# Two expert stages: when the second tile is turned, how long unread products run, and when the last quarter of a weight matrix is loaded

## The chip, the cores and the metric

The kernel runs on one core of a Trainium2 chip, as one program. The metric is the device time of one execution in microseconds (us). TensorE is called PE, VectorE DVE, ScalarE ACT, GpSimd POOL and SyncE SP, as in the profile.

## The reference, cut to what matters

Two transformer layers over x of 4096 tokens by 256 channels, each an attention and a feed-forward part made of eight experts. Every token goes to one expert. Only the feed-forward parts matter here:

```python
# layer 0: every token to the centroid that scores it highest
aff = x @ centroids.T; assign = argmax(aff, 1); alpha = sigmoid(aff[assign])
h = relu(layernorm(x, ln_g[e], ln_b[e]) @ w1[e].T + b1[e])     # 256 -> 1024
ye = x + h @ w2[e].T + b2[e]                                   # 1024 -> 256
out = alpha * ye + (1 - alpha) * x
# layer 1: top-capacity selection, then for the expert of each token
h = gelu(x @ W1[e]) @ W2[e]                                    # 256 -> 512 -> 256
out = weight * h
```

All of it is in float32.

## The kernel before, in words

The tokens are sorted by expert on the chip. For each layer a *plan* finds the place of each token and inverts the sorting: `invert_dve` builds one-hot matrices on DVE in four batches, and `invert_pe` multiplies them on PE, batch after batch, each waiting on `p_low`. The result, read by DVE in `keep_tokens`, is `tok_i`: which token sits in which row of which 128-row tile. Then comes an *expert stage*, a software pipeline over tiles (39 in layer 0 in `expert_stage`, 34 in layer 1 in `f1_*`). All engines run their own instruction streams in program order and meet through semaphores.

For tile j the work is: POOL fetches 128 rows of 3 KB from DRAM by `tok_i` (indirect DMA, L1173 and L1899; at most six tiles ahead); PE turns the rows (`turn_in`, two transposes, L1198 and L1916); ACT copies the turned rows to SBUF (L1359, with scale and bias; L1979 in layer 1); DVE copies the first matrix of the tile's expert into `w_now` (L1303, 128x2048; L2016 in layer 1); PE multiplies (`up`, 32 matmul records, L1210; 16, L1932); ACT applies relu (L1365) or gelu (L1987); PE multiplies by the second matrix (`down`, L1224, L1955), read in place from `whi` in layer 0; DVE adds, scales and normalises; POOL stores.

In layer 0, PE's program order at the start is: turn 0, up 0, turn 1, turn 2, up 1, down 0, up 2, down 1, and so on. Because `w_now` is a single buffer, DVE refills it for tile 1 in two halves: the first when half of up 0 is done (L1297, semaphore `half`), the second when all of it is (L1303). ACT's order is: copy 0, copy 1, relu 0, copy 2, relu 1. In layer 1, `w_now1` is double, and the order is: turn 0, up 0, turn 1, turn 2, up 1, down 0.

`hold_clock(n)` issues n matmuls of the identity into a bank that nobody reads, which the profile records as 2n matmuls of line L287. It stands before the stage (25 in both layers) and before `invert_pe` (30 in layer 0, 34 in layer 1).

SP issues all direct DMAs in one program order, on one queue. `whi` takes the second matrices of layer 0 (1 MB for an expert) in six loads on the semaphore `s_w2`: experts 0, 1, 2 and 4 during the attention, and in `plan0_sync` expert 3 and then experts 5 to 7 in one load of 3 MB. Behind them, once the last normalised rows are stored, come four loads on `s_bias`: two scale and shift vectors, the first bias `b1T`, and the second bias spread over 128 partitions (`b2bc`, 1 MB, L1078). Then SP waits for the third turned tile (`tin` at 3) and loads the next layer's weights. `waits0` says what each stream waits for as it starts: DVE for `s_bias` and the first matrices (`s_w1`), ACT for `s_bias`, PE ahead of down 0 for all of `s_w2`.

Of the kernel before, what the change touches and what calls it, by code (L numbers as in the profile page):

```python
# [68 lines left out]
def two_layer_kernel(nc, a):  # L69
    ctx = ExitStack()  # L70
    with ctx:
# [66 lines left out]
        s_x, s_cst, s_w1, s_w2, s_wa, s_wb, s_modbc = (sem(n) for n in ("s_x", "s_cst", "s_w1", "s_w2", "s_wa", "s_wb", "s_modbc"))  # L138
# [27 lines left out]
        dve = {}  # L166
# [146 lines left out]
        def batches(count):  # L313
            return min(count, B)

        W2_LOADS = 6

        def load_w2(eng, e, count=1):

# [750 lines left out]
        def plan0_sync(eng):  # L1070
            eng.wait_ge(ev["aff"], scored(B - 1))
            load_w2(eng, 3)
            load_w2(eng, 5, 3)
            eng.wait_ge(s_fin, 16 * (2 + 2 * B))
            eng.dma_start(g0T, a["ln_gT"]).then_inc(s_bias, 16)
            eng.dma_start(be0T, a["ln_bT"]).then_inc(s_bias, 16)
            eng.dma_start(b1T, a["b1T"]).then_inc(s_bias, 16)
            eng.dma_start(b2bc, a["b2"].unsqueeze(0).broadcast_to([P, E, D])).then_inc(s_bias, 16)  # L1078

        def plan0_vector(eng):  # L1080
            ch = dve["chain"]
# [54 lines left out]
        def expert_stage(layer, tag, cv, cx, src_d, dst_d, rounds_before, w_up, w_down, nf, prep_in, hidden_act, bias_row, waits):  # L1136
# [48 lines left out]

            def on_tensor(eng):
                waits(eng, "tensor")
                hold_clock(eng, 25)
                eng.wait_ge(p_tok, layer + 1)

                def turn_in(t):
                    if normed and t.by_blocks():
                        return
                    eng.wait_ge(s_in[t.slot], (t.rounds + 1 + rounds_before[t.slot]) * 16)
                    if t.after(1):
                        eng.wait_ge(e_["inT"], t.j - 1 if normed and t.after(3) else t.j)
                    for c in range(C):
                        last = eng.transpose(b_in[:, c * P:(c + 1) * P], xin[t.slot][:, c * P:(c + 1) * P], ident)  # L1198
                    last.then_inc(e_["tin"], 1)

                def up(t):
                    eng.wait_ge(e_["inT"], t.j + 1)
                    eng.wait_ge(e_["w"], t.j + (2 if t.after(1) else 1))
                    if t.after(2):
                        eng.wait_ge(e_["act"], t.j - 1)
                    for f in range(nf):
                        if t.static and t.j == 1 and f == nf // 2:
                            eng.wait_ge(e_["w"], 3)
                        for c in range(C):
                            last = eng.matmul(b_up[t.par][f // 4][:, (f % 4) * P:(f % 4 + 1) * P], w_now[:, c, f * P:(f + 1) * P],  # L1210
                                              inT[t.par][:, c * P:(c + 1) * P], start=c == 0, stop=c == C - 1)
                        if t.static and t.j == 0 and f == nf // 2 - 1:
                            last.then_inc(e_["half"], 1)
                    last.then_inc(e_["up"], 1)

                def down(t):
                    e = expert_of(eng, t)
                    eng.wait_ge(e_["act"], t.j + 1)
                    if not t.after(1):
                        waits(eng, "down")  # L1220
                    if t.after(2):
                        eng.wait_ge(e_["sum"], t.j - 1)
                    for f in range(nf):
                        last = eng.matmul(b_dn[t.par][:, 0:D], hidT[t.par][:, f * P:(f + 1) * P],  # L1224
                                          w_down[:, bass.ds(e, 1), f, :].rearrange("p o n -> p (o n)"),
                                          start=f == 0, stop=f == nf - 1)
                    last.then_inc(e_["dn"], 1)
                def turn_rest(t):
                    if not t.static or t.j != 1:
                        turn_in(t)  # L1230

                def turn_second(t):
                    if t.static and t.j == 1:
                        turn_in(t)
                pipeline(eng, [(ahead, turn_rest), (ahead + 1, up), (ahead, turn_second), (ahead + 2, down)], head)

            def on_scalar(eng):
                eng.wait_ge(p_tok, layer + 1)
# [32 lines left out]
            def on_vector(eng):  # L1271
# [33 lines left out]
                def out_rows(t):  # L1305
                    total = fout[t.par][:, wide - D:wide]
                    ffn = b_dn[t.par][:, 0:D]
                    if normed:
                        e = expert_of(eng, t)
                    eng.wait_ge(e_["dn"], t.j + 1)  # L1310
                    eng.wait_ge(s_in[t.slot], (t.rounds + 1 + rounds_before[t.slot]) * 16)
                    if t.after(2):
                        eng.wait_ge(s_st[t.par], t.pairs * 16)
                    settle(eng)
                    if normed:
                        eng.tensor_tensor(total, ffn, bias_row(e), ALU.add).then_inc(e_["b"], 1)
                        eng.wait_ge(e_["b"], t.j + 1)
                        settle(eng)
                        ffn = total
                    eng.scalar_tensor_tensor(total, ffn, slot_w[:, bass.ds(t.j, 1)], xin[t.slot][:, 2 * D:], ALU.mult, ALU.mult).then_inc(e_["y"], 1)  # L1320
                    eng.wait_ge(e_["y"], t.j + 1)
                    eng.tensor_tensor(total, total, xin[t.slot][:, D:2 * D], ALU.add).then_inc(e_["sum"], 1)
                    if normed:
                        st_, mv_, _ = ln[t.par]
                        eng.wait_ge(e_["sum"], t.j + 1)
                        settle(eng)
                        eng.bn_stats(st_, total).then_inc(e_["bs"], 1)
                        eng.wait_ge(e_["bs"], t.j + 1)
                        settle(eng)
                        eng.bn_aggr(mv_, st_).then_inc(e_["mv"], 1)  # L1330
# [13 lines left out]
        def waits0(eng, who):  # L1344
            if who == "sync":
                eng.dma_start(wqkv1, a["wqkv1"]).then_inc(s_wa, 16)
                for k in range(TB):
                    eng.dma_start(wfc[k * 32:(k + 1) * 32].rearrange("r j n -> r (j n)"), a["wfc"]).then_inc(s_wa, 16)
                eng.dma_start(wg, a["wg"]).then_inc(s_wa, 16)
            elif who in ("vector", "scalar"):  # L1350
                eng.wait_ge(s_bias, 64)
                if who == "vector":
                    eng.wait_ge(s_w1, 16)
            elif who == "down":
                eng.wait_ge(s_w2, 16 * W2_LOADS)

# [550 lines left out]
        def f1_tensor(eng):  # L1907
# [11 lines left out]
            def up(t):  # L1919
                eng.wait_ge(g_["inT"], t.j + 1)  # L1920
                wait_some(eng, g_["act"], t.j - 1)
                if t.mixed:
                    eng.wait_ge(g_["unit"], 2 * STRIPS * (t.nth + 1))
                    for c in range(C):
                        for k, u in enumerate(t.strips):
                            last = eng.matmul(b_up1[t.par][u, :], inT1[t.par][:, c * P + u.start:c * P + u.stop], unit_up[t.nth % 2][:, k, c, :],  # L1926
                                              start=c == 0, stop=c == C - 1)
                else:
                    eng.wait_ge(g_["w"], t.full + 1)
                    for f in range(NF1):  # L1930
                        for c in range(C):
                            last = eng.matmul(b_up1[t.par][:, f * P:(f + 1) * P], w_now1[t.full % 2][:, c, f * P:(f + 1) * P],  # L1932
                                              inT1[t.par][:, c * P:(c + 1) * P], start=c == 0, stop=c == C - 1)
                last.then_inc(g_["up"], 1)
# [24 lines left out]
            def step(at):  # L1959
                now, second, third, fourth = (at(lag) for lag in range(4))  # L1960
                if now and now.j != 1:
                    turn_in(now)
                if second:
                    up(second)
                if now and now.j == 1:
                    turn_in(now)
                if fourth and fourth.mixed:
                    down(fourth)
                if third:
                    (turn_hidden if third.mixed else down)(third)  # L1970
# [88 lines left out]
        with nc.Block() as block:  # L2059
# [5 lines left out]

            @block.vector
            def _(eng):
                ch = Chain(eng, "s_vq")
                ch.do(eng.tensor_reduce(mx, key3, AX.X, ALU.max))
                eng.tensor_tensor(key3, key3, bc_last(mx, E), ALU.subtract).then_inc(q_key, 1)  # L2070
                for i, n in enumerate(ODD + EVEN + (0,)):
# [71 lines left out]
            def _(eng):  # L2143
# [19 lines left out]
                hold_clock(eng, 18)  # L2163
                eng.wait_ge(p_one, 2)
                prefix_pe(eng, onehot, p_pre)
                hold_clock(eng, 34)
                invert_pe(eng, 1).then_inc(p_inv, 1)
                f1_tensor(eng)

# [54 lines left out]
```

## Time and profile before

| | |
|---|---|
| three timed runs | 1011.42, 1015.40, 1015.35 us; median 1015.35 |
| profiled execution | 1017.07 us, span of the core 1015.1 us |
| mean granted PE clock | 0.975 |
| busy share of the span | PE 93%, weight loads 78%, DVE 69%, ACT 48%, POOL 32% |
| layer 0's expert stage | first rows fetched at 226.3 us, last products about 496 us |
| layer 1's expert stage | first rows fetched at 862.9 us, end of the span 1015.1 us |

The span runs from the first to the last instruction of the profiled execution; the 1.97 us between it and that execution's time lie outside the instructions. Times in the timelines are counted from the span's start. A granted clock of 1.00 is 2.4 GHz, 0.50 is 1.2 GHz.

### The profile page before, as it was taken

To read this page: it belongs to the slowest core of one execution; us is meant where nothing else is said; L and a number is where in the kernel's file an instruction comes from. 1 tells how busy PE (TensorE), PEld (TensorE's weight loads), DVE (VectorE), ACT (ScalarE), POOL (GpSimd) and SP (SyncE) were. 2 spreads that over 40 slices of the span, in tenths; PEclk is the share of its full clock that TensorE was granted. 3 is DMA by queue.
4 is the path that set the end of the run, shared out by engine and by line. 5 is a ranking of instruction groups with operands and counts; after the bars stand their busy time and mean duration, and the time that the engine had idled before them with its cause. 6 is when DMAs were issued, how large, how long until landed. Compare 5 with 4: busy or idle time off the path is not lost. (4 is left out here: it accounts for less than half of the span.)

```text
span 1015.1 us, 29867 instructions
## 1 busy us (share of the span) xinstructions
PE 941.4 (93%) x11226; PEld 793.5 (78%) x11227; DVE 705.3 (69%) x1820; ACT 491.7 (48%) x1325; POOL 321.5 (32%) x288
## 2 busy tenths in 40 slices
PE   6899999987999999999999999999878889999996
PEld 3466666887999999999987778888767778888875
DVE  3567887873777777777640679899888777466662
ACT  3646565312545444454534868788762440222221
POOL 0034533612232323323120334434433000555562
PEclk9999999998999999999999999999999897999998
DMA  9884581285322223222116757766642710443440
GB/s 337 233 329 120 126 269 70 85 309 192 95 89 85 90 88 98 78 94 87 45 40 117 132 104 156 144 148 141 118 106 70 310 65 1 138 135 117 140 139 32
DMA packets 130474, 133.76 MB, mean 132 GB/s; under 512 B 73693, under 2 KB 118879, under 8 KB 128181
## 3 DMA queue, kind: packets, MB, share of 16 engines
q1 hardware_dynamic: 119764, 90.82, 32.3%
q0 software_dynamic: 10592, 41.30, 12.7%
q8 instruction: 82, 1.34, 0.6%
q14 instruction: 36, 0.29, 0.1%
HBM read 94.27 MB, written 44.11 MB: 136 GB/s over the span
## 5 line engine op out<-in xcount | busy, mean ns | idle before, releaser
L1210 PE MATMUL psall<-rows 128*128 128x128 f32 x1248 | 148.2, 278 | 1.7 <-DVE rows L1303 1.7
L1210 PEld LDWEIGHTS psall<-rows 128*128 128x128 f32 x1248 | 146.3, 195 | 2.9 <-ACT rows L1359 1.9
L1224 PE MATMUL psall<-whi,rows 128*128 x624 | 141.0, 379 | 0.0
L1224 PEld LDWEIGHTS psall<-whi,rows 128*128 128x128 f32 x624 | 115.7, 190 | 14.1
L1178 POOL DMA_INDIRECT attn_rows<-rows,tok_i x39 | 41.7, 1069 | 183.6 <-DVE rows L1335 183.6
L287 PE MATMUL psall<-cst 128*128 128x128 f32 x718 | 93.8, 289 | 0.6 <-PEq L1451 0.6
L1570 DVE STREAM_TRANSPOSE whi<-whi 32x512 f32<-32x512 f32 x128 | 89.9, 702 | 5.9 <-POOL whi L1529 3.8
L287 PEld LDWEIGHTS psall<-cst 128*128 128x128 f32 x718 | 89.5, 204 | 1.4 <-issue 1.1
L1303 DVE COPY rows<-wlo 128x2048 f32 (+1 forms) x39 | 47.3, 1214 | 58.1 <-PE psall L1210 49.4
L1365 ACT ACTIVATE rows<-psall,vs 128x128 f32<-128x128 f32 x312 | 84.6, 382 | 4.5 <-PE psall L1210 2.1
L1649 ACT ACTIVATE whi<-psall 32x512 f32<-32x512 f32 x128 | 75.1, 587 | 12.7 <-PE psall L1814 10.5
L1899 POOL DMA_INDIRECT x<-ffn_rows,tok_i x34 | 38.8, 1142 | 123.2 <-DVE tok_i L1057 74.3
L1741 PE MATMUL psall<-wlo,x 128*32 128x128 f32 x2048 | 65.6, 280 | 2.0 <-issue 1.9
L1741 PEld LDWEIGHTS psall<-wlo,x 128*32 128x32 f32 x2048 | 56.1, 113 | 12.0 <-issue 11.1
L1266 ACT ACTIVATE small<-small,eps_t 128x1 f32<-128x1 f32 x39 | 11.5, 295 | 107.0 <-DVE small L1330 107.0
L1529 POOL TENSOR_TENSOR whi<-whi,wlo 128x512 f32<-128x512 f32 x32 | 34.0, 1063 | 89.5 <-DVE wlo L1561 89.5
L773 PE MATMUL psall<-whi 128*128 128x512 f32 x128 | 58.0, 597 | 1.1 <-ACT key L679 1.1
L1173 POOL DMA_INDIRECT x<-ffn_rows,tok_i x39 | 40.0, 1025 | 52.8 <-issue 34.1
L1932 PE MATMUL psall<-rows 128*128 128x128 f32 x448 | 54.7, 275 | 0.5 <-ACT rows L1979 0.5
L1955 PE MATMUL psall<-wlo,rows 128*128 x224 | 54.0, 385 | 0.0
L1932 PEld LDWEIGHTS psall<-rows 128*128 128x128 f32 x448 | 52.3, 192 | 0.8 <-ACT rows L1979 0.8
L1979 ACT ACTIVATE rows<-psall 128x256 f32<-128x256 f32 x34 | 13.1, 385 | 78.1 <-PE psall L1916 78.1
(299 smaller groups left out, 1842.7 us busy)
## 6 DMA issues: line engine op xcount, KB each, us to landing
ffn_rows<-mod_rows SPq DMA_DIRECT2D x2, 4096.0 KB
wlo<-attn_rows SPq DMA_DIRECT2D x64, 128.0 KB, 3.3
wlo<-in_W SPq DMA_DIRECT2D x2, 4096.0 KB, 17.7
whi<-in_w SPq DMA_DIRECT2D x5, 1024.0 KB, 8.7
whi<-mod_rows SPq DMA_DIRECT2D x4, 1024.0 KB, 14.0
ffn_rows<-rows SPq DMA_DIRECT2D x8, 512.0 KB
ffn_rows<-x SPq DMA_DIRECT2D x8, 512.0 KB
v_turn<-wlo SPq DMA_DIRECT2D x32, 128.0 KB, 3.2
```

Source lines behind the costliest of these rows:

```text
L287: eng.matmul(b_idle, ident, ident, start=True, stop=True)
L773: last = eng.matmul(ps[k % 2][:, :], h0T[:, c, k * P:(k + 1) * P], wqkv[:, c, D:3 * D], start=c == 0, stop=c == C - 1)
L1178: eng.indirect_dma_start(dst_d, bass.IndirectOffsetOnAxis(tok_i[:, j:j + 1].bitcast(U32), 0), fout[j % 2], None, bounds_check=T - 1, oob_i ...
L1210: last = eng.matmul(b_up[t.par][f // 4][:, (f % 4) * P:(f % 4 + 1) * P], w_now[:, c, f * P:(f + 1) * P], inT[t.par][:, c * P:(c + 1) * P], ...
L1224: last = eng.matmul(b_dn[t.par][:, 0:D], hidT[t.par][:, f * P:(f + 1) * P], w_down[:, bass.ds(e, 1), f, :].rearrange("p o n -> p (o n)"), ...
L1303: eng.tensor_copy(w_now[:, :, part], w_of_e[:, :, part]).then_inc(e_["w"], 1)
L1365: last = eng.activation(dst[:, f * P:(f + 1) * P], banks[f // 4][:, (f % 4) * P:(f % 4 + 1) * P], ACT.Relu, bias=b1T[:, f, bass.ds(e, 1)])
L1570: last = eng.transpose(ebd[t % 2][rows_q, :, 32 * q:32 * q + 32], sc[t % 3][rows_q])
L1649: last = eng.activation(sc[t % 3][rows_q], b_s[rows_q, :, 32 * q:32 * q + 32], ACT.Copy)
L1741: last = eng.matmul(b_qk[t % 2][k * QD:(k + 1) * QD, n * P:(n + 1) * P], wqkv1[:, c, h * QD:(h + 1) * QD], hT[b % 2][:, c, k * P:(k + 1) * ...
L1932: last = eng.matmul(b_up1[t.par][:, f * P:(f + 1) * P], w_now1[t.full % 2][:, c, f * P:(f + 1) * P], inT1[t.par][:, c * P:(c + 1) * P], st ...
L1955: last = eng.matmul(b_dn1[t.par][:, 0:D], hidT1[t.par][:, f * P:(f + 1) * P], w_down1[:, bass.ds(e, 1), f, :].rearrange("p o n -> p (o n)" ...
```

## The change

1. `plan0_sync` loads expert 5 alone. Experts 6 and 7 (2 MB, "the last quarter") are asked for after the four bias loads and after a wait for the rows of tile 1 (`s_in[1]`). There are seven loads on `s_w2`.
2. Layer 0's stage holds with 30 unread products, not 25; layer 1's plan with 40, not 34. The hold of 25 at the start of layer 1's stage stays.
3. In both stages tile 1 is turned in the middle of up 0, not after it.
4. DVE no longer waits for `s_bias` as it starts the stage; it does so ahead of its first output rows (`out`).
5. The second plan's DVE chain uses the first one's semaphore.

```diff
-        W2_LOADS = 6
+        W2_LOADS = 7
...
             load_w2(eng, 3)
-            load_w2(eng, 5, 3)
+            load_w2(eng, 5)
             eng.wait_ge(s_fin, 16 * (2 + 2 * B))
...
             eng.dma_start(b2bc, a["b2"].unsqueeze(0).broadcast_to([P, E, D])).then_inc(s_bias, 16)
+            eng.wait_ge(s_in[1], 16)
+            load_w2(eng, 6, 2)
...
                 waits(eng, "tensor")
-                hold_clock(eng, 25)
+                hold_clock(eng, 30)
                 eng.wait_ge(p_tok, layer + 1)
...
                     for f in range(nf):
+                        if t.static and t.j == 0 and f == nf // 2:
+                            turn_in(Tile(0, 1))
                         if t.static and t.j == 1 and f == nf // 2:
                             eng.wait_ge(e_["w"], 3)
...
-                def turn_second(t):
-                    if t.static and t.j == 1:
-                        turn_in(t)
-                pipeline(eng, [(ahead, turn_rest), (ahead + 1, up), (ahead, turn_second), (ahead + 2, down)], head)
+                pipeline(eng, [(ahead, turn_rest), (ahead + 1, up), (ahead + 2, down)], head)
...
                     eng.wait_ge(e_["dn"], t.j + 1)
+                    if not t.after(1):
+                        waits(eng, "out")
...
-            elif who in ("vector", "scalar"):
+            elif who == "vector":
+                eng.wait_ge(s_w1, 16)
+            elif who in ("scalar", "out"):
                 eng.wait_ge(s_bias, 64)
-                if who == "vector":
-                    eng.wait_ge(s_w1, 16)
...
                     for f in range(NF1):
+                        if t.j == 0 and f == NF1 // 2:
+                            turn_in(Packed(1))
...
                 if second:
                     up(second)
-                if now and now.j == 1:
-                    turn_in(now)
...
-                ch = Chain(eng, "s_vq")
+                ch = dve["chain"]
...
-                hold_clock(eng, 34)
+                hold_clock(eng, 40)
                 invert_pe(eng, 1).then_inc(p_inv, 1)
```

## Rows read from the trace of the kernel before

**Rows 1.** Page, costliest groups: line, form, count | busy, mean ns | idle before.
```profile
...
L1210 PE MATMUL psall<-rows 128*128 128x128 f32 x1248 | 148.2, 278 | 1.7 <-DVE rows L1303 1.7
...
```

**Rows 2.** Timeline, layer 0: start, duration us, engine, line, form [idle before].
```profile
...
220.41 2.01 PE L1049 MATMUL psall<-rows 128*128 128x78 f32 x16 [0.24 <-DVE rows L1034]
...
220.88 0.43 SPq L1078 DMA_DIRECT2D x<-in_b  x1
...
224.50 5.79 PE L287 MATMUL psall<-cst 128*128 128x128 f32 x50
...
226.33 1.20 POOL L1173 DMA_INDIRECT x<-ffn_rows,tok_i  x1 [21.15 <-issue]
227.84 1.01 POOL L1173 DMA_INDIRECT x<-ffn_rows,tok_i  x1 [0.30 <-issue]
...
233.09 0.41 PE L1198 MATMUL psall<-cst,x 128*128 128x128 f32 x2 [2.80 <-DMA x<-ffn_rows,tok_i]
233.76 0.81 ACT L1359 ACTIVATE rows<-psall,vs 128x128 f32<-128x128 f32 x2 [24.17 <-PE psall L1198]
233.81 1.27 DVE L1303 COPY rows<-wlo 128x2048 f32 x1 [8.73 <-issue]
...
235.23 6.22 PE L1210 MATMUL psall<-rows 128*128 128x128 f32 x32 [1.73 <-DVE rows L1303]
...
241.65 0.69 DVE L1303 COPY rows<-wlo 128x1024 f32 x1 [1.78 <-PE psall L1210]
...
243.08 3.74 PE L1210 MATMUL psall<-rows 128*128 128x128 f32 x32
...
246.66 3.62 PE L1224 MATMUL psall<-whi,rows 128*128 x16
...
```

**Rows 3.** Line L1173's fetches of rows from 220 to 240 us.
```profile
...
DMA to landing us min/median/max: 4.6/5.6/6.6
...
```

**Rows 4.** Line L1899's fetches of rows from 850 to 900 us.
```profile
...
DMA to landing us min/median/max: 3.9/4.3/4.7
...
```

**Rows 5.** DMA issues, 205 to 262 us: KB each, us to landing.
```profile
...
whi<-in_w SPq DMA_DIRECT2D x1, 3072.0 KB, 14.7
...
```

**Rows 6.** Windows: us; PE, PEld, DVE, ACT, POOL busy; clock, DMA, GB/s.
```profile
...
224.00:226.00 2.00, 2.00 (x20) 2.00 (x19) 0.30 (x2) 0.00 (x0) 0.00 (x0) 1.00 0.94 406
234.00:236.00 2.00, 0.77 (x3) 0.80 (x4) 1.08 (x1) 0.56 (x2) 0.06 (x1) 0.50 0.90 289
240.00:242.00 2.00, 1.67 (x14) 1.43 (x12) 0.35 (x1) 0.12 (x1) 0.00 (x0) 0.93 0.00 0
...
```

**Rows 7.** Timeline, entry of layer 1's expert stage, columns as in rows 2.
```profile
...
840.39 7.75 PE L287 MATMUL psall<-cst 128*128 128x128 f32 x68
...
849.06 12.58 PE L1049 MATMUL psall<-rows 128*128 128x68 f32 x64 [0.92 <-DVE rows L1034]
...
854.66 0.72 DVE L1034 TENSOR_TENSOR rows<-rows,token_weight 128x544 f32<-128x544 f32 x1
...
857.60 0.18 DVE L1017 TENSOR_SCALAR tile_expert<-extra 128x24 int32<-128x24 f32 x1
...
861.43 7.47 PE L287 MATMUL psall<-cst 128*128 128x128 f32 x50
...
861.86 0.18 DVE L1057 TENSOR_SCALAR tok_i<-psall 128x34 int32<-128x34 f32 x1
...
862.86 1.52 POOL L1899 DMA_INDIRECT x<-ffn_rows,tok_i  x1 [74.30 <-DVE tok_i L1057]
...
868.74 0.38 PE L1916 MATMUL psall<-cst,x 128*128 128x128 f32 x2
...
872.74 1.95 PE L1932 MATMUL psall<-rows 128*128 128x128 f32 x16
...
874.53 1.89 PE L1955 MATMUL psall<-wlo,rows 128*128 x8
...
```

**Rows 8.** Windows, layer 1, columns as in rows 6.
```profile
...
852.00:854.00 2.00, 2.00 (x12) 2.00 (x11) 2.00 (x4) 0.00 (x0) 0.00 (x0) 0.50 0.00 0
...
```

## The prediction

> **What bounds the kernel now.** I read the page's groups first. Line L1210, the up products of layer 0's expert stage, has 148 us of work in 1248 records and only 1.7 us of idle time ahead of it [rows 1]: once the pipeline is full, PE never waits, so whatever brings PE earlier into its stream is kept to the end. The change touches only how the two stages are entered, so I read the two entries in the timeline, instruction by instruction, then the clock windows over them.
>
> Entry of layer 0 [rows 2]. PE's 50 unread products end at 224.50 + 5.79 = 230.29. The first rows are asked for at 226.33, but PE turns them only at 233.09, released by the DMA, 6.6 us after the request; that is the longest landing of the six first fetches, whose shortest is 4.6 [rows 3]. Layer 1's fetches land in 3.9 to 4.7 us, 4.3 in the middle [rows 4]. The difference is load: the DMA engines are 0.94 busy and move 406 GB/s as the fetches begin [rows 6], with the 3 MB load, which takes 14.7 us [rows 5], and b2bc, issued at 220.88, still queued. DVE's copy of `w_now` begins at 233.81 after 8.73 us of idle time that no engine ended: it is the wait for `s_bias`. It ends at 235.08, and up 0 starts at 235.23. ACT had ended at 233.76 + 0.81 = 234.57. So two waits end almost together: biases, then rows. Because PE was idle but for two transposes for 4.9 us, its clock has fallen to 0.50 in the window from 234, and is back only in the window from 240 (0.93) [rows 6]: up 0 takes 6.22 us, where up 1, at full clock, takes 3.74. Then a gap: up 0 ends at 241.45, up 1 starts at 243.08. Down 0 starts at 246.66 with PE dense from there.
>
> Entry of layer 1 [rows 7]. The 68 unread products end at 848.14, the first batch of the inversion starts at 849.06, and all 64 products take 12.58 us, ending at 861.64, because the clock is at 0.50 [rows 8]. At full clock 16 such products take 2.01 us in layer 0 [rows 2]. DVE had its last batch ready at 854.66 + 0.72 = 855.38 and its other work done at 857.78. `tok_i` is written at 861.86, rows are asked for at 862.86, and turn 0 at 868.74 stands right behind the hold, which the low clock stretched to 7.47 us.
>
> **The change in layer 0.** *Biases.* 2 MB (2.10 million bytes) leave the queue ahead of b2bc; at 406 GB/s that is 5.2 us [rows 6]. DVE's copy, now without that wait, runs at about 226 under the hold: cost nothing, covered by the hold, 1.27 us if the cover went. ACT still waits for `s_bias`. The copy's release at 233.81 puts the biases at about 233 now, so about 228 then, ahead of the rows. *Rows.* With the queue drained I take layer 1's 4.3 us, so tile 0 lands at 230.6; ends 3.9 (230.2) and 6.6 (232.9) [rows 3, 4]. *Hold.* 60 products at 0.116 us end at 224.50 + 6.95 = 231.45: the hold now ends after the rows, and turn 0 starts at 231.5, 1.6 us before 233.09. The five more holds cost about 0.9 us against the rows. Turn 0 to ACT's end took 1.48 us and PE follows 0.15 later, so up 0 starts at 233.1, a gain of 2.1. *Clock.* PE is then idle for some 1.2 us, not 4.9; I take the full clock, a gain of 6.22 - 3.74 = 2.5; the other end is no gain. *Turn amid.* Two transposes of 0.41 busy, pipelined into the stream, add 0.25 (0.2 to 0.4). They need tile 1's rows: 227.84 + 4.3 = 232.1, against 235.0 when PE gets there. ACT's copy 1 and DVE's two half copies (0.69 each) then lie under the rest of up 0 and the first half of up 1. The gap of 1.63 us before up 1 shrinks to turn 2's 0.25: a gain of 1.4. The sum is 2.1 + 2.5 - 0.25 + 1.4 = 5.7: PE could start down 0 at 241.0.
>
> *The last quarter.* SP issues it at about 232.2. From below: an unloaded fetch of 0.39 MB takes 3.9 us, of which 1.0 is its bytes at 406 GB/s, so 2.9 fixed and 5.2 for 2 MB: 240.3. Four fetches, 1.3 us apart behind the one at 227.84, still have some of their 1.6 MB in flight; I add 1.6 us, 241.9. From above, the 14.7 us of the 3 MB load: 246.9 [rows 5]. I take 241.9, nearer the low end since nothing is queued in front. Queued behind it on SP are only the next layer's weights, which nobody needs for 250 us; behind PE's wait at down 0 stands everything. So down 0 starts at 242.0, and the gain of the stage is 4.7 (0 to 6.3).
>
> The Trainium skill ("DMA: Bandwidth & Descriptors", Queues, rings and completion order) says that each DMA engine goes round the queues that have work, packet by packet. It speaks against this part: the quarter and the fetches would stretch each other. By it, the rows of tiles 2 to 5 take up to all their 1.6 MB out of the load's time, 4.0 us rather than my 1.6, down 0 at 244.4 and the time 1008.4, inside the first case below. The landings of [rows 3] against [rows 4] agree in direction.
>
> **The change in layer 1.** 12 more records at 0.114 us make the plan's hold end at 849.5, 0.45 after the first batch is ready. PE then runs 4 batches of 2.0 us without a break: 857.5; DVE's last batch alone gives 855.38 + 2.0 = 857.4. So the late start costs 0.1, if the clock holds, and the inversion ends 4.1 earlier. DVE's other work ends at 857.78, so `tok_i` is 3.9 earlier, at 858.0. Rows land at 862.86 - 3.9 + 4.3 = 863.3, and 50 unread products at full clock (5.8) end at 863.4. Turn 0 is at 863.6, a gain of 5.1. From turn 0 to up 1 took 4.0 us; with tile 1 turned amid, up 0's 1.95 and its start at turn 0 + 0.9, it takes 0.9 + 1.95 + 0.5 = 3.4: 0.6 more (0 to 0.8). ACT's gelu of tile 0 must now fit under turn 2 and up 1, 2.2 us from the end of up 0; down 0 stands at 874.53, 2.8 after up 0's end as it is reckoned from these rows (868.74 + 0.9 + 2.05), so at most 0.6 shows, and I take off 0.2. The gain is 5.5. If the clock had been kept before too, only 1 of it is left.
>
> The shared semaphore costs nothing: the chain's instructions and waits are the same, and none of them overlaps another chain.
>
> **Sum.** Against the profiled execution: 1017.07 - 4.7 - 5.5 = 1006.9. That execution is 1.7 above the median of the runs shown; the same subtraction from the median is 1005.2. The three runs lie 4 us apart, which is the size of the layer 1 clock loss: 1011.42 looks like an execution that kept it, and from that one 4.7 + 1 leads to 1005.7. I say 1006.0.
>
> **Rivals.** *A, as worked out:* 1002 to 1009; chance 0.57. *B, the clock falls all the same.* After the hold ends, gaps of one microsecond remain, and the inversion's products are narrow (68 columns). For it: in layer 1 it fell after a gap of 0.92 us ahead of such products [rows 7]; against it: layer 0's inversion, with gaps of 0.24 and 78 columns, kept it. Price 4.1 in layer 1 (1010) or 2.5 in layer 0 (1008.5), both 1012.5; chance 0.17. The Trainium skill ("TensorE: Matmul & The Clock Gate", A second HAM failure mode) tells of a kernel that loses the clock again and again through such short gaps; this trace agrees for layer 1's inversion alone. *C, the quarter is the new wait:* landing as slowly as 3 MB did, down 0 starts at 246.9, all of layer 0's gain is gone: 1010.7; chance 0.12. *D, the loss in layer 1 is rare:* the kernel before runs mostly as in 1011.42, and side by side the gain is about 5.7, 0.56%, or little less; the time is still 1006, but the verdict can be none; chance 0.09. *E, slower:* the quarter's place decides: it is asked for only after tile 1's rows, so a load that starts or lands late stalls PE at down 0 one for one. It would have to land 14 us after 242, at 256, 24 us after its issue, to make 1020.4. Against it is that 3 MB with more in front took 14.7. Chance 0.05.
>
> **How the numbers follow.** About 0.5%, 5 us, is what a measurement of this kernel tells from no change. A, half or more of B, a part of C and D end over 0.5% faster: 0.74; the rest of B, C and D within 0.5%: 0.21; slower 0.05. The range goes from 1001.5 (A's lower end, with other dips of the clock missing) to 1011.5 (B and C).
>
> **What would show it.** Right: in layer 0 turn 0 at 231.5 behind 60 unread products, copy L1303 under them, up 0 in about 4.0 us, L1198 in its middle, up 1 within 0.3 us of its end, down 0 released by the DMA of `whi` at 241 to 243. In layer 1, an inversion of about 8.0 us at clock 1.00 and turn 0 five microseconds sooner. Wrong: a clock of 0.50 in either place; PE waiting several microseconds at down 0; rows of tile 1 not there in the middle of up 0; idle time ahead of L1210 later in the stage, which would mean that DVE or the stores, not PE, set its pace.

## The result, and the profile after

The changed kernel takes 1007.0 us (median of four runs, 1006.17 to 1008.64), the kernel before 1014.23 (four runs, 1011.42 to 1015.4). The ratio is 0.9927, 95% interval 0.9904 to 0.995: 7 us faster, with 1006.0 forecast. The profiled execution of the changed kernel took 1006.78 us, its span 1004.8. The forecast number is right, but half of the way to it is not: of the two gains it is made of, 4.7 us in layer 0 and 5.5 in layer 1, the first isn't there.

The page's groups of the changed kernel, in the columns of [rows 1]. The down products (L1228; L1224 in the kernel before, with 0.0 us of idle time ahead of them) now have 3.8 us of it ahead of them, ended by a DMA:

```profile
...
L1228 PE MATMUL psall<-whi,rows 128*128 x624 | 142.8, 383 | 3.8 <-DMA whi<-in_w 3.8
...
```

The timeline of the changed kernel at the entry of layer 0's stage, the counterpart of [rows 2]:

```profile
...
224.39 6.91 PE L287 MATMUL psall<-cst 128*128 128x128 f32 x60
...
225.91 1.23 DVE L1303 COPY rows<-wlo 128x2048 f32 x1 [0.95 <-issue]
...
231.24 0.41 PE L1200 MATMUL psall<-cst,x 128*128 128x128 f32 x2
231.88 0.81 ACT L1361 ACTIVATE rows<-psall,vs 128x128 f32<-128x128 f32 x2 [22.40 <-PE psall L1200]
...
232.74 2.05 PE L1214 MATMUL psall<-rows 128*128 128x128 f32 x16 [1.09 <-ACT rows L1361]
...
233.07 0.33 SPq L321 DMA_DIRECT2D whi<-in_w  x1
...
234.63 0.38 PE L1200 MATMUL psall<-cst,x 128*128 128x128 f32 x2
...
235.75 0.69 DVE L1297 COPY rows<-wlo 128x1024 f32 x1 [8.62 <-PE psall L1214]
...
236.99 0.69 DVE L1303 COPY rows<-wlo 128x1024 f32 x1 [0.55 <-PE psall L1214]
...
237.84 3.81 PE L1214 MATMUL psall<-rows 128*128 128x128 f32 x32 [0.66 <-DVE rows L1303]
...
245.41 5.40 PE L1228 MATMUL psall<-whi,rows 128*128 x16 [3.77 <-DMA whi<-in_w]
...
250.65 3.73 PE L1214 MATMUL psall<-rows 128*128 128x128 f32 x32
...
```

Up to the end of up 0 all is as forecast. The unread products end at 231.3, turn 0 starts at 231.24 (231.5 forecast), DVE's copy lies under the hold at 225.91, up 0 starts at 232.74 at full clock (1.00 in every window from 224 to 246), with tile 1's transposes at 234.63 in its middle. Up 1 starts at 237.84, 5.2 us earlier than in [rows 2], but 1.0 after the end of up 0, where at most 0.3 was forecast: it waits for DVE's second half copy, which runs from 236.99 to 237.68. It ends at about 241.6, and then PE waits for 3.77 us: down 0 starts at 245.41, released by the DMA of `whi`, and takes 5.40 us instead of 3.62. Up 2 starts at 250.65; in the kernel before it was 250.11. The loads of the changed kernel (KB, us from issue to landing) and its clock windows (columns as in rows 6):

```profile
...
whi<-in_w SPq DMA_DIRECT2D x1, 2048.0 KB, 12.1
...
x<-in_wqkv SPq DMA_DIRECT2D x1, 768.0 KB, 8.8
...
```

```profile
...
242.00:244.00 2.00, 0.00 (x0) 0.00 (x0) 1.93 (x5) 2.00 (x8) 0.00 (x0) 1.00 1.00 415
...
246.00:248.00 2.00, 2.00 (x8) 1.69 (x7) 0.00 (x0) 0.00 (x0) 0.00 (x0) 0.69 1.05 225
248.00:250.00 2.00, 2.00 (x6) 1.55 (x6) 0.00 (x0) 0.00 (x0) 0.00 (x0) 0.50 0.59 126
...
```

The quarter, issued at 233.07, lands after 12.1 us, with the DMA engines full up to then (415 GB/s in the window from 242). While PE waits the clock is still granted in full; it falls after 246, and most of down 0 runs at 0.50.

The timeline of the changed kernel at the entry of layer 1's stage, the counterpart of [rows 7], and a clock window of it:

```profile
...
836.86 10.72 PE L287 MATMUL psall<-cst 128*128 128x128 f32 x80
...
847.41 7.26 PE L1049 MATMUL psall<-rows 128*128 128x68 f32 x64
...
854.51 5.80 PE L287 MATMUL psall<-cst 128*128 128x128 f32 x50
...
854.89 0.18 DVE L1057 TENSOR_SCALAR tok_i<-psall 128x34 int32<-128x34 f32 x1
...
855.88 1.53 POOL L1901 DMA_INDIRECT x<-ffn_rows,tok_i  x1 [71.14 <-DVE tok_i L1057]
...
861.10 0.41 PE L1918 MATMUL psall<-cst,x 128*128 128x128 f32 x2 [0.79 <-DMA x<-ffn_rows,tok_i]
...
862.05 1.16 PE L1936 MATMUL psall<-rows 128*128 128x128 f32 x8 [0.54 <-ACT rows L1981]
...
864.37 1.95 PE L1936 MATMUL psall<-rows 128*128 128x128 f32 x16
...
866.16 1.89 PE L1959 MATMUL psall<-wlo,rows 128*128 x8
...
```

```profile
...
838.00:840.00 2.00, 2.00 (x11) 2.00 (x11) 1.79 (x12) 0.00 (x0) 0.00 (x0) 0.50 0.00 0
...
```

The inversion now takes 7.26 us at full clock, not 12.58. In the kernel before, the first 2.2 us of the inversion still ran at full clock:

```profile
...
850.00:852.00 2.00, 1.88 (x14) 1.74 (x14) 2.00 (x4) 0.00 (x0) 0.00 (x0) 0.82 0.00 0
...
```

The 0.82 of this window is full clock until about 851.3 and 0.50 from there; the next windows are at 0.50 throughout [rows 8], so the other 10.4 us of the inversion ran at half. In the changed kernel the clock did fall, but earlier, in the unread products (0.50 from 838), which stretch to 10.72 us; it is back at 1.00 from 842, before they end (847.58), and they end after the first batch is ready (845.5). Turn 0 follows at 861.10 and down 0 at 866.16.

Where the span's 10.3 us went, from the same events in both timelines: up 2 of layer 0 starts 0.54 later. From there to the hold ahead of layer 1's inversion, code that the change doesn't touch, is 4.07 shorter (840.39 - 250.11 against 836.86 - 250.65). From that hold to turn 0 is 4.11 shorter, from turn 0 to down 0 0.73, and from down 0 to the end 1.93. Together 10.3. The runs below ask which of these are the change's.

### The profile page after: what moved, and what is told of

It is laid out like the page before. It is cut to its first block and busy times, and to the rows that moved or that the text cites. A ratio compares the mean times of both kernels' runs of the same rounds, so it can differ in the third digit from the quotient of the medians.

```text
span 1004.8 us, 29913 instructions
## 1 busy us (share of the span) xinstructions
PE 937.9 (93%) x11248; PEld 789.5 (79%) x11249; DVE 705.6 (70%) x1820; ACT 492.1 (49%) x1325; POOL 321.8 (32%) x288
## 5 line engine op out<-in xcount | busy, mean ns | idle before, releaser
L1214 PEld LDWEIGHTS psall<-rows 128*128 128x128 f32 x1248 | 144.0, 192 | 3.2 <-ACT rows L1361 1.3
L1228 PE MATMUL psall<-whi,rows 128*128 x624 | 142.8, 383 | 3.8 <-DMA whi<-in_w 3.8
L1228 PEld LDWEIGHTS psall<-whi,rows 128*128 128x128 f32 x624 | 116.8, 192 | 18.6 <-issue 4.0
L287 PE MATMUL psall<-cst 128*128 128x128 f32 x740 | 97.5, 291 | 0.9 <-PEq L1453 0.9
L287 PEld LDWEIGHTS psall<-cst 128*128 128x128 f32 x740 | 93.0, 205 | 1.7 <-issue 1.4
L1651 ACT ACTIVATE whi<-psall 32x512 f32<-32x512 f32 x128 | 75.1, 587 | 13.8 <-PE psall L1816 11.5
L1266 ACT ACTIVATE small<-small,eps_t 128x1 f32<-128x1 f32 x39 | 11.5, 295 | 113.9 <-DVE small L1332 113.9
L1743 PEld LDWEIGHTS psall<-wlo,x 128*32 128x32 f32 x2048 | 54.5, 110 | 12.1 <-issue 11.5
L1936 PEld LDWEIGHTS psall<-rows 128*128 128x128 f32 x448 | 52.4, 192 | 1.8 <-issue 0.9
L1959 PEld LDWEIGHTS psall<-wlo,rows 128*128 128x128 f32 x224 | 40.4, 190 | 11.9 <-issue 7.5
```

The source lines that it names most:

```text
L287: eng.matmul(b_idle, ident, ident, start=True, stop=True)
L1651: last = eng.activation(sc[t % 3][rows_q], b_s[rows_q, :, 32 * q:32 * q + 32], ACT.Copy)
L1743: last = eng.matmul(b_qk[t % 2][k * QD:(k + 1) * QD, n * P:(n + 1) * P], wqkv1[:, c, h * QD:(h + 1) * QD], hT[b % 2][:, c, k * P:(k + 1) * ...
L1959: last = eng.matmul(b_dn1[t.par][:, 0:D], hidT1[t.par][:, f * P:(f + 1) * P], w_down1[:, bass.ds(e, 1), f, :].rearrange("p o n -> p (o n)" ...
```

## The experiments

The theory after the first trace: (1) the whole gain comes from keeping the clock in layer 1's inversion; (2) in layer 0 the last quarter lands late and takes back what the earlier rows, the clock and the turning give; (3) the 4 us in code that isn't changed are chance. The rival: the layer 0 entry gains as forecast on the whole, and its stall is one execution's chance.

Each block ran on one chip, beside the kernel before. The column "entry" is from the start of layer 0's hold (L287) to the start of up 2, in the profiled execution; it is 25.61 us before. The kernel of r7_hold40_alone has the layer 0 code of the kernel before, so its 24.30 is a second reading of that.

| run | median us | ratio to before (95%) | entry |
|---|---|---|---|
| r1_change_again | 1009.23 | 0.9929 (0.9912 to 0.9945) | 25.74 |
| r2_loads_undone | 1007.77 | 0.9926 (0.9901 to 0.9950) | 23.46 |
| r3_hold34 | 1013.95 | 0.9971 (0.9951 to 0.9991) | 26.85 |
| r4_own_semaphore | 1004.84 | 0.9883 (0.9861 to 0.9905) | 20.70 |
| (before, same chip) | 1015.81 | | |
| r5_own_turn_undone | 1004.22 | 0.9901 (0.9870 to 0.9933) | 20.74 |
| r6_own_hold25 | 1004.85 | 0.9903 (0.9871 to 0.9934) | 22.03 |
| r7_hold40_alone | 1008.96 | 0.9947 (0.9920 to 0.9974) | 24.30 |
| r8_quarter_at_once | 1007.08 | 0.9927 (0.9899 to 0.9954) | 23.92 |
| (before, same chip) | 1014.29 | | |
| r9_quarter_later | 1010.28 | 0.9951 (0.9929 to 0.9974) | 27.35 |
| r10_own_again | 1004.86 | 0.9885 (0.9856 to 0.9914) | 20.52 |
| r11_eighth_last | 1005.82 | 0.9907 (0.9873 to 0.9941) | 21.43 |
| r12_eighth_half | 1004.29 | 0.9876 (0.9845 to 0.9908) | 21.68 |
| (before, same chip) | 1016.21 | | |

**The changed kernel again.** No edit.

> The changed kernel once more, beside the runs it is to be compared with. Theory (the last quarter of the second weights lands late and stalls TensorE at the first down products; the gain lies elsewhere): 1007 us as before, down 0 waits 3 to 4 us for the load. Rival (the gain over the kernel before is the entry of layer 0, the stall is one execution's chance): down 0 starts at 241 to 242 us here and the time is about 1002 us.

The stall is there again: down 0 at 245.41 after 3.22 us of idle time, 5.40 us long. The rival falls. The entry takes 25.74 us, where the changed kernel's first trace has 26.26; r3_hold34, with the changed code in layer 0 too, has 26.85. The old code has 25.61 and, in r7_hold40_alone, 24.30: no gain in layer 0, if anything a loss of 0.1 to 2.6 us.

**The last quarter on a semaphore of its own.** The load stays where the change puts it; only PE's wait moves, from down 0 to down 2. This relies on the inputs: the first two tiles hold tokens of an expert whose weights are there.

```diff
-            load_w2(eng, 6, 2)
+            load_w2(eng, 6, 2, s_w2_last)
...
+                    if t.static and t.j == 2:
+                        waits(eng, "down_last")
```

> The changed kernel with the last quarter on a semaphore of its own, waited for ahead of the third tile's down products and not ahead of the first's (with these inputs the first tiles are of experts whose weights are there). Theory: down 0 starts right behind up 1, at 241.7 us, at full clock; the third tile's up products start at 245.4 instead of 250.65 us, and the time is 1001.8 us. Rival (something else than the quarter holds the pipeline, the gathers or the next layer's weights): the stall moves to another instruction and the time stays within 1 us of 1007.

PE's timeline in that kernel:

```profile
...
231.95 0.41 PE L1200 MATMUL psall<-cst,x 128*128 128x128 f32 x2
...
238.55 3.81 PE L1214 MATMUL psall<-rows 128*128 128x128 f32 x32 [0.82 <-DVE rows L1305]
242.19 3.62 PE L1230 MATMUL psall<-whi,rows 128*128 x16
245.65 3.73 PE L1214 MATMUL psall<-rows 128*128 128x128 f32 x32
...
```

Down 0 starts right behind up 1 and takes 3.62 us, and the entry is 5.0 us shorter than the changed kernel's on the same chip; the median is 4.4 us lower (1004.84 against 1009.23; the 1001.8 of the expectation counted from 1007.0, which the changed kernel doesn't reach on this chip). No other wait takes the place of the one removed, and the gain is kept: the stage's last up products start at 506.0 us, at 511.0 in the changed kernel. The repetition in the last block,

> The kernel with the last quarter on its own semaphore, once more, for comparison on this chip: 1004 to 1005 us, ratio 0.988 to 0.990, down 0 at 241.6 to 242.2 us behind up 1 without a stall.

gives 1004.86 us and an entry of 20.52 (down 0 at 243.84, because the hold itself begins 1.8 us later). So the quarter's lateness costs the changed kernel some 5 us, of which 3.1 to 3.8 are PE's wait and 1.8 the slow down 0; in r3_hold34, where the clock fell sooner, it is 3.0:

```profile
...
245.37 6.63 PE L1228 MATMUL psall<-whi,rows 128*128 x16 [3.08 <-DMA whi<-in_w]
...
```

**The loads undone.**

```diff
-            load_w2(eng, 5)
+            load_w2(eng, 5, 3)
...
-            eng.wait_ge(s_in[1], 16)
-            load_w2(eng, 6, 2)
```

> The changed kernel with the loads of the kernel before (experts 5 to 7 in one load of 3 MB, six loads). Theory: the biases and first rows come at 233 us again, up 0 starts at 235 and is slow again, but nothing stalls down 0: the third tile's up products start at about 248.5 us where the changed kernel has 250.65, and the time is 1005 us, 1 to 2 us below the changed kernel. Rival (the split of the loads is what gains): 4.7 us slower than the changed kernel, 1011.5 us.

```profile
...
232.98 0.41 PE L1198 MATMUL psall<-cst,x 128*128 128x128 f32 x2 [1.50 <-DMA x<-ffn_rows,tok_i]
234.48 3.42 PE L1212 MATMUL psall<-rows 128*128 128x128 f32 x16 [1.09 <-ACT rows L1359]
...
248.04 3.73 PE L1212 MATMUL psall<-rows 128*128 128x128 f32 x32
...
```

The rows come late again (turn 0 at 232.98), the clock falls in up 0 (3.42 us for half of it), but nothing stalls down 0. The entry is 2.3 us shorter than in the repeated change, the median 1.5 lower; the ratios can't be told apart. So as it stands the split of the loads doesn't pay.

**Layer 1's hold undone, and alone.** Here `hold_clock(eng, 40)` ahead of `invert_pe(eng, 1)` is 34 again, or the kernel before gets the 40 and nothing else.

> The changed kernel with 34 unread products ahead of layer 1's inversion, as before. Theory: the clock falls in the inversion in some executions and costs 4.1 us there, so the runs spread from 1007 to 1011 us, median about 1009.5, at least 1.5 us above the changed kernel. Rival (the holds do nothing, the clock in the inversion is chance in both kernels): same median within 1 us, and the same spread as the changed kernel.

> The kernel before with 40 unread products ahead of layer 1's inversion and nothing else. Theory (this is where the whole gain of the change comes from): the inversion takes 7 to 8 us at full clock, 4 us below the kernel before, ratio 0.995 to 0.996. Rival (each other part adds its share too): half of that or less, ratio above 0.9975, and the inversion is at half clock in spite of the longer hold.

PE's timeline in the changed kernel with 34, one of its clock windows, and PE's timeline in the kernel before with 40:

```profile
...
840.96 7.75 PE L287 MATMUL psall<-cst 128*128 128x128 f32 x68
849.64 12.39 PE L1049 MATMUL psall<-rows 128*128 128x68 f32 x64 [0.92 <-DVE rows L1034]
...
```

```profile
...
854.00:856.00 2.00, 2.00 (x11) 2.00 (x11) 2.00 (x5) 0.00 (x0) 0.00 (x0) 0.50 0.00 0
...
```

```profile
...
846.56 8.11 PE L1049 MATMUL psall<-rows 128*128 128x68 f32 x64
...
```

With 34 the gap of 0.92 us and the slow inversion are back (12.39 us; the clock falls 2.4 us into it), the median is 4.7 us higher, more than the expected 1.5 to 2.5, and twelve runs spread from 1006.37 to 1017.10; six of the changed kernel lie between 1006.31 and 1009.97. With 40 alone, the inversion takes 8.11 us and the ratio is 0.9947: 5.3 us of gain in medians. In all twelve profiled executions of kernels with 40 the inversion takes 7.26 to 8.13 us; in both with 34, more than 12. From the start of the hold to turn 0 both kernels with 34 take 28.35 us and the twelve with 40 take 23.10 to 24.78: 3.6 to 5.3 us less, the size of the medians' 4.7 and 5.3. But 40 is not the whole gain: with 34 the changed kernel is still faster than the kernel before (0.9971, 0.9951 to 0.9991; 1.9 us in medians, 0.9 to 5.0 by the interval). Turning amid in layer 1 gives 0.7 of that in the traces; for the rest they show no place. Against 40 alone (0.9920 to 0.9974) the whole change (0.9912 to 0.9945) can't be told apart.

The change's shared semaphore has no run of its own. In the traces it moves nothing: DVE's first batch of the inversion is ready 8.6 us after the hold's start in both kernels (849.01 - 840.39 and 845.47 - 836.86).

**Tile 1 turned after up 0 again**, in both stages, on top of the own semaphore, because in the changed kernel itself the stall would hide it.

```diff
-                        if t.static and t.j == 0 and f == nf // 2:
-                            turn_in(Tile(0, 1))
...
-                        if t.j == 0 and f == NF1 // 2:
-                            turn_in(Packed(1))
```

> The kernel with the last quarter on its own semaphore, and tile 1 turned after up 0 again, in both stages. Prediction's sizes (turning amid gains 1.15 us in layer 0 and 0.6 in layer 1): 1.8 us slower than with it. Rival, from the trace of the changed kernel: up 1 waits for the second half of its weights, which DVE copies only after up 0, so turning amid gains just 0.3 us in layer 0 and 0.6 to 0.9 in layer 1: 1 us slower, and up 1 starts at 238.8 to 238.9 us where it started at 238.55.

```profile
...
231.09 0.41 PE L1200 MATMUL psall<-cst,x 128*128 128x128 f32 x2
...
241.63 3.62 PE L1228 MATMUL psall<-whi,rows 128*128 x16
...
```

Turn 0 to down 0 takes 10.54 us, against 10.24 with the turn amid (241.63 - 231.09 and 242.19 - 231.95): 0.30. In layer 1 it is 5.82 against 5.06: 0.76. The rival's sizes are met, the forecast's 1.15 for layer 0 is not. The medians, on two chips, differ by less than they spread.

**25 unread products in layer 0**, on top of the own semaphore.

> The kernel with the last quarter on its own semaphore, and 25 unread products at the start of layer 0's stage. Theory (the hold of 30 ends after the rows have landed and costs, the clock is safe with either): turn 0 starts when the rows land, at 230.9 to 231.2 instead of 231.9 us, up 0 at full clock, up to 1 us faster. Rival (the shorter hold lets the clock fall in some executions): the same or up to 1.5 us slower, with a clock of 0.50 in up 0 or up 1.

```profile
...
224.42 5.79 PE L287 MATMUL psall<-cst 128*128 128x128 f32 x50
231.12 0.41 PE L1200 MATMUL psall<-cst,x 128*128 128x128 f32 x2 [0.91 <-DMA x<-ffn_rows,tok_i]
...
242.99 3.62 PE L1230 MATMUL psall<-whi,rows 128*128 x16
...
```

The rows are there no earlier: turn 0 comes 6.70 us after the hold's start, where the hold of 60 products lasts 6.91. PE has been idle for 0.91 us, the clock falls in the middle of up 0 (0.87 in the window from 232, 0.50 in that from 234) and turn 0 to down 0 takes 11.87 us, not 10.24. So in the traces five more products cost 0.1 to 0.3 us and save 1.6 where the clock would fall. How often it falls with 25 is open: the profiled execution is the slowest of its six (1008.26), which spread over 5.4 us, those of the own semaphore over 2.0 and 2.1, but the medians are the same (1004.85 against 1004.84 and 1004.86).

**The quarter at once, behind the biases.** The line `eng.wait_ge(s_in[1], 16)` is left out.

> The changed kernel, with the last quarter asked for right behind the biases, without the wait for tile 1's rows. Theory (the lateness is the wait; the DMA engines have time between the biases and the rows): the quarter is there by 236 us, rows land 0.5 to 1 us later than in the changed kernel, down 0 starts at 242 to 243 us, 4 us below the changed kernel. Rival (the quarter in front of the rows delays them as in the kernel before): turn 0 at 233 us, up 0 partly at half clock, third tile's up products at 248 us, 2 us below the changed kernel.

```profile
...
225.23 6.91 PE L287 MATMUL psall<-cst 128*128 128x128 f32 x60
233.84 0.41 PE L1199 MATMUL psall<-cst,x 128*128 128x128 f32 x2 [1.71 <-DMA x<-ffn_rows,tok_i]
235.35 3.66 PE L1213 MATMUL psall<-rows 128*128 128x128 f32 x16 [1.09 <-ACT rows L1360]
...
245.70 3.62 PE L1227 MATMUL psall<-whi,rows 128*128 x16
...
```

The rival is right on the entry: turn 0 comes 8.61 us after the hold's start, as in the kernel before (8.59), up 0's first half takes 3.66 us, and the entry is 23.92. The ratio, 0.9927, is the changed kernel's, so the 2 us of the rival, let alone the 4 of the theory, don't show in the time; the interval leaves room for the 2. Lateness is exchanged for a delay of the rows.

**The quarter later**: `s_in[3]` for `s_in[1]`.

> The changed kernel, with the last quarter asked for two fetches later (after tile 3's rows, not tile 1's). Theory (the landing of the quarter alone sets down 0): issue 2.6 us later, with fewer rows beside it the load itself 1 to 1.5 us shorter, so down 0 starts 1 to 2 us later, at 246.5 to 247.5 us, and the third tile's up products at 251.5 to 252.5: 1 to 2 us slower than the changed kernel. Rival (total bytes set the landing, not the moment of the request): down 0 and the time as in the changed kernel, within 0.5 us.

```profile
...
233.01 0.41 PE L1200 MATMUL psall<-cst,x 128*128 128x128 f32 x2
...
246.96 6.77 PE L1228 MATMUL psall<-whi,rows 128*128 x16 [3.54 <-DMA whi<-in_w]
253.56 1.61 PE L1214 MATMUL psall<-rows 128*128 128x128 f32 x13
...
```

```profile
...
whi<-in_w SPq DMA_DIRECT2D x1, 2048.0 KB, 8.7
...
```

Turn 0 to down 0 is 13.95 us, against 14.17 and 13.63 in the changed kernel's two traces, although the request was 3.1 us later against turn 0: the load took 8.7 us, not 12.1 or 11.5. Here the rival is right, and my slope was wrong. The bytes fit this. Between request and landing the DMA engines moved 4.25 MB in the changed kernel, at 351 GB/s: 2.10 of the quarter, 1.24 of fetches, 0.90 of the next layer's weights. Here they moved 3.18 MB at 366 GB/s: 2.10, 0.38 and 0.70. What is in flight altogether goes with the landing; no run changed the bytes alone. The time, 0.9951, isn't shown to be worse than the changed kernel's 0.9929: the intervals overlap. The entry's 27.35 us has a down 0 of 6.77 at the fallen clock, but r3_hold34 has 6.63 with the load where the change puts it, so that isn't shown to come from the later request.

**One eighth due, the other MB not.** Experts 5 and 6 early; behind tile 1's rows expert 7, then `b2bc` on its own semaphore for DVE's first output rows. This needs nothing of the inputs.

```diff
-            load_w2(eng, 5)
+            load_w2(eng, 5, 2)
...
             eng.wait_ge(s_in[1], 16)
-            load_w2(eng, 6, 2)
+            load_w2(eng, 7)
+            eng.dma_start(b2bc, a["b2"].unsqueeze(0).broadcast_to([P, E, D])).then_inc(s_b2, 16)
...
+            elif who == "scalar":
+                eng.wait_ge(s_bias, 48)
+            elif who == "out":
+                eng.wait_ge(s_b2, 16)
```

> The changed kernel with another order of the loads: experts 5 and 6 early, then the three small bias loads, then after tile 1's rows expert 7 alone (1 MB) and the spread second bias (1 MB), which only DVE's first output rows wait for, on its own semaphore. TensorE waits for all eight experts at down 0 as in the changed kernel. Theory: the same 2 MB go ahead of the rows, but only half the late bytes are due at down 0; expert 7 lands by 240 to 241 us, no stall, the second bias by 246, down 0 at 241.7 to 242.5 us; as fast as the kernel with its own semaphore, 4 to 5 us below the changed kernel. Rival (it is the late start, not the size): expert 7 lands after 244 us, a stall of 2 us or more remains.

And on top of it, up 1 starts on the first half of its weights:

```diff
-                    eng.wait_ge(e_["w"], t.j + (2 if t.after(1) else 1))
+                    eng.wait_ge(e_["w"], t.j + (2 if t.after(2) else 1))
```

> The kernel of the run before, and up 1 starts as soon as the first half of its weights is copied (its second half waits for the second copy, as the code already does in the middle). Theory: up 1 starts 0.8 to 0.9 us sooner behind turn 2, and down 0 too if expert 7 has landed by 241 us: 0.5 to 0.9 us faster in the trace, which these rounds can hardly tell. Rival (the wait for the second half only moves into the middle of up 1, or the load is the next wait): nothing gained.

PE's timeline in the first of these kernels, and in the second:

```profile
...
232.22 0.41 PE L1200 MATMUL psall<-cst,x 128*128 128x128 f32 x2
...
243.35 3.72 PE L1228 MATMUL psall<-whi,rows 128*128 x16 [0.72 <-DMA whi<-in_w]
...
```

```profile
...
231.31 0.41 PE L1200 MATMUL psall<-cst,x 128*128 128x128 f32 x2
...
236.93 3.74 PE L1214 MATMUL psall<-rows 128*128 128x128 f32 x32
242.50 3.72 PE L1228 MATMUL psall<-whi,rows 128*128 x16 [1.84 <-DMA whi<-in_w]
...
```

Expert 7's 1 MB takes 9.0 and 9.1 us. In the first it lands at 243.1, between the theory's 240 to 241 and the rival's 244; a stall of 0.72 us is left, and the clock holds. In those 9.0 us the engines moved 3.11 MB: 1.05 of expert 7, 1.27 of fetches and 0.77 of what stands behind it on the same queue, so the load doesn't have that queue to itself. With the early start, up 1 begins 0.2 us behind turn 2 instead of 1.2, but the stall grows to 1.84: the load is the next wait, as the rival says, and the entry is no shorter (21.68 against 21.43). Their medians are 1005.82 and 1004.29 us where the kernel before takes 1016.21. The first one's interval still overlaps the changed kernel's; the second's, 0.9845 to 0.9908, lies below the 0.9912 to 0.9945 of the repeated change, which ran on another chip. It is the fastest version of the study that asks nothing of the inputs, and can't be told from the own semaphore at 0.9885.

## Why the prediction was right, and where not

*The bound.* Right: PE sets the pace once the pipeline is full. The 0.54 us at up 2 are still there when the stage's last up products start (510.5 us before, 511.0 after; the stage's last products run to 517, not to about 496).

*Layer 0, biases, rows, hold, clock.* Right, and in size: the biases landed at 227.1 for 228, turn 0 1.85 us earlier for 1.6, up 0 2.5 earlier for 2.1, up 0 at full clock. The rows' 4.3 us were nearer 4.9: the 25-product run shows them there 0.2 us before the longer hold ends.

*The turn amid.* The mechanism was right, the size in layer 0 was not: 0.30 us, not 1.15. The step that failed is "the gap of 1.63 us before up 1 shrinks to turn 2's 0.25". The prediction put ACT's copy of tile 1 and both half copies under products, the second half copy under the first half of up 1. But up 1 waits for both halves of `w_now` before its first product, and DVE copies the second half after up 0; the idle 0.82 us in front of up 1 in the own-semaphore kernel is released by DVE. The run with the early start removes it. In layer 1, with two buffers, it was 0.73 for the 0.4 that the forecast took (0.6 less 0.2). A slip beside it: the stage's upper bound of 6.3 has down 0 at 240.3, before PE could be ready by the prediction's own 241.0; it should have been 5.7. The 1020.4 of the case "slower" should be 1020.0 by its own 14 us.

*The last quarter.* This is the step that failed: "I add 1.6 us, 241.9". The load takes 12.1 us, not 9.7, and lands at 245.2. The 1.6 us stood for 0.65 MB of fetches, and the next layer's weights behind the quarter were put at nothing, "which nobody needs for 250 us". The trace has 1.24 MB of fetches and 0.90 MB of these weights moved before the quarter landed; at the 351 GB/s of that stretch this is, as an estimate, 3.5 and 2.6 us. The weights are there because of the change itself: SP asks for them behind the third turned tile, at 237.25, while in the kernel before this came at 243.32, with no load of `whi` left. The later request, which lands at about the same time after turn 0, agrees: the landing follows all that is in flight. The rule of the Trainium skill that the prediction weighed ("DMA: Bandwidth & Descriptors", Queues, rings and completion order: each engine goes round the queues that have work) gave 244.4 for down 0 and was nearer to the measured 245.41. The trace agrees in that load and fetches share the engines; but the 1.6 MB of fetches that the 244.4 counted were 1.24, and the weights, which it left out, made up for them, so its closeness is in part luck. On top came what neither had: PE's clock fell about 1.4 us after down 0 had begun, 1.8 us. The entry lost 0.5 us instead of gaining 4.7. So the rival "the quarter is the new wait" is what happened in layer 0, at about the place where it was put (down 0 at 246.9).

*Layer 1.* Right in mechanism: the inversion keeps the clock, so the rival of a clock that falls all the same fails where it was put, in all twelve traces with 40. From the hold to turn 0 the forecast was 5.1 and the trace has 4.1: the rows came 5.2 us after their request (4.3 forecast), 0.8 after the hold's end, and the clock, falling in the hold itself, made it 1.6 us longer, so that the inversion began late. Four of the twelve traces with 40 have that; the other eight have a hold of 9.09 us. The runs don't show why. The runs with 34 and with 40 alone put 4.7 and 5.3 us on this hold, medians on one chip each; the whole change gains 6.6 to 7.2. That the loss is rare in the kernel before, the prediction's fourth case, doesn't fit: both traces with 34 have it, and the medians move by its size.

*Why the number came out.* The profiled execution of before stood 1.7 us above the median of its runs, and 4.07 us of its distance to the one after lie in untouched code. That is chance: two profiled executions of one and the same kernel, the own semaphore, need 598.35 and 595.00 us from up 2 to the inversion (844.00 - 245.65 and 842.29 - 247.29). Over all fourteen traces the stretch from up 2 to that hold takes 585.5 to 590.4 us, whatever the edit. The 1.93 us in layer 1's remaining tiles are of the same kind: r4_own_semaphore, whose code there is the changed kernel's, needs 139.44 from down 0 to the end of its span, the changed kernel 138.64, the kernel before 140.57; r7_hold40_alone, with the old code there, has 140.83 and r6_own_hold25, with the new, 141.1. So the 1006.0 owes something to luck. Its sum began at 1017.07, 2.8 above the median that the kernel before has over four runs, and counted a gain of 4.7 that isn't there; without both it would have been 1014.23 - 5.5 = 1008.7, and 1007.0 was measured. In medians the change is worth 6.6 to 7.2 us, of which layer 1's hold has about 5; for the remaining 2 the run with 34 leaves 0.9 to 5.0, and the traces place only 0.7 of them; where the rest comes from stays open.

What stays open: whether the quarter would land 2.6 us sooner without the next layer's weights, as their bytes suggest. It was not tried to hold those back, which would be the next run.

## What to carry to other kernels

A load that is moved to make room for something comes due at its own consumer: price its landing from all bytes in flight at its request and behind it, not from its own size, and compare with the time at which the consumer becomes ready after the gain, not before. Let only those wait for a late load who read it, and give it its own semaphore. If PE's clock is at stake, unread products should last until the work is surely there: in these traces the surplus cost tenths of a microsecond and a fallen clock 1.6 to 5 us.

## What the runs showed of the hardware

- In both kernels with 34 the inversion began after a gap of 0.92 us and the clock fell 2.2 and 2.4 us into it. It then stayed at 0.50 to the inversion's end, some 10 us in which PE was busy, and came back only 3.5 and 3.9 us into the next unread products [rows 7, 8]. With the first batch directly behind the hold, it fell in none of twelve inversions.
- At layer 0's entry PE waits 1.1 to 1.7 us between turn 0 and up 0. In the nine traces in which turn 0 stood right behind the hold and this was the only wait (1.09 us), up 0 ran at full clock, 3.8 to 4.0 us of products. In the five in which PE had also waited 0.91 to 2.80 us for the rows, the clock fell before up 0's end, and its products took 5.3 to 6.2 us.
- The cost of an idle stretch comes after it. In the changed kernel PE stood still from 241.6 to 245.4 at full granted clock, and the clock fell at about 246.8, under down 0 (5.40 us). How late varies: in r3_hold34 and r9_quarter_later it had fallen 0.6 to 0.9 us before down 0 began, and down 0 took 6.63 and 6.77.
- In one queue, the landing time of a load doesn't follow its size: 1 MB with another MB behind it took 9.0 us, 2 MB took 8.7 to 12.1. It followed the bytes that all queues moved meanwhile: 3.11 MB in 9.0 us, 3.18 in 8.7, 4.25 in 12.1, at 347 to 366 GB/s.
